# Four column groups for the weighted values, and layer norms worked out beside products, in an eight-stage kernel

## The chip, the cores and the metric

The kernel runs on one core of a Trainium2 chip. The metric is the device time of one launch in microseconds (us), median over runs. The core's engines are named as the profile names them: PE (TensorE; PEld is its loading of weights), DVE (VectorE), ACT (ScalarE), POOL (GpSimd) and SP, which issues the DMA transfers. Each engine works through its own list of instructions in order and waits only at semaphores.

## What is computed

The residual `x` holds 8 batches of 128 rows (tokens) of 512 columns. Four layers each add a gated attention and a gated feed-forward part, each over the layer norm of `x`:

```python
x = x + tanh(g_xattn[0]) * L0_xattn(layernorm(x), ctx, mask, ...)
x = x + tanh(g_ffn[0])   * L0_ffn(layernorm(x), w1, w2, w3)
x = x + tanh(g_xattn[1]) * L1_xattn(layernorm(x), ctx, ctx)
x = x + tanh(g_ffn[1])   * L1_ffn(layernorm(x), W_org, lora_down, lora_up, lora_keys, Wq)
x = x + tanh(g_xattn[2]) * L2_xattn(layernorm(x), ctx, Wq, Wk, Wv, Wo)
x = x + tanh(g_ffn[2])   * L2_ffn(layernorm(x), W_base, b_base, W_router, A, B)
# layer 3 in the same manner; the change does not touch it
```

The parts that the change touches, with their sizes:

- L0 attention (the "first attention"): 4 windows of 128 columns per batch, 8 heads of width 8; scores 128 x 128 per head and window, masked softmax, `o = attn @ v`, then gelu, an output projection 64 -> 128 and the mask.
- L0 feed-forward (the "first feed-forward stage"): `silu(h w1) * (h w2)`, then `@ w3`, hidden width 1376; only its end is touched.
- L1 feed-forward (the second): `h @ W_org` plus eight low-rank experts of rank 64; each batch's weights come from a softmax over the 8 expert keys for the mean row of that batch.
- L2 attention (the third): 16 query heads of width 96 over 4 key/value heads; keys and values from 128 context rows followed by the batch's own 128 rows ("latents").
- L2 feed-forward (the third): `h @ W_base + b_base` plus the two best of eight experts of rank 16.

## The kernel before

Eight stages run one after another, each a function; the change touches `l0_attention`, `l0_ffn`, `l1_ffn`, `l2_attention` and `l2_ffn`. Between stages all engines meet at a barrier and the semaphores are cleared. Most stages begin with `layernorm_all` (L129 to L214): it turns row statistics, which the stage before gathers behind each update of `x` (`row_stats`, L105), into means and variances of all eight batches (L135), takes the power -1/2 on POOL (L170), normalises on DVE, and, where the stage wants the rows transposed, has PE transpose each batch (L185, L194) and ACT copy it (L204). The order of work on each engine is written out by hand; `after(engine, semaphore, value)` is a wait.

**L0 attention.** A step works on batch b and prepares batch b + 1. PE projects queries and keys (`proj`, four tiles g), makes the scores twice: once with queries on the rows (`scores`, L411 and L416), from which DVE takes the maxima (L598), and once transposed (`scores_t`, L436 to L443), which ACT exponentiates (L527) into `pt`. The maxima are turned by PE (L423) and cast by DVE (L601), and that cast starts the next step's transposed scores. The weighted values are `pv` (L453): per head k and window n one product with a 128 x 128 weight tile, cut out of `vpad` so that head k's eight values and eight ones lie in the rows that belong to k; all heads add up in one bank, rows 0 to 63 numerators and 64 to 127 denominators. ACT copies the bank out (L542), and DVE takes reciprocals of 64 rows and multiplies (`second`, L571, L573), once per batch. `pt` has four slots, so later exponentials wait for `pv` of earlier heads. A last block takes gelu per batch, projects and updates `x`.

**L1 feed-forward.** Per pair of batches: POOL copies the transposed rows into `hs` (L1278), PE makes the low-rank "down" products per batch in 128 columns (L1290), the router's products (L1295, L1301), then the outputs (L1306 the base, L1309 the low-rank part) in 512 columns; DVE scales the low-rank values, updates `x` and gathers statistics.

**L2 attention.** A cycle of `step` handles the weighted values of batch b and the projections of b + 1. Weighted values (L1640): for each of four key/value heads r, four query heads g and two parts (context, latents), one product with the probabilities as 128 x 128 weights and 97 columns of values and ones; DVE takes four reciprocals and one product per r (L1815, L1817) into `o`, PE transposes `o` in twelve tiles (L1651), ACT copies them (L1737) to `o_t`, and the output products (L1661) follow. DVE also rounds the weights of the last stage here (`rounding`), beside everything else.

**L2 feed-forward.** Per batch four base products (L1957), one product of a row of ones with the bias (L1958), a transposition (L1960) and the expert product (L1962); POOL copies the rows (L1937) and, behind the last of these, scales weights of the next stage (L2065).

## Time and profile before

| | us |
|---|---|
| median of 3 runs | 1694.49 (1693.63 to 1696.26) |
| the profiled execution, its own time | 1687.38 |
| its span | 1685.6 |
| PE busy | 1444.7 |
| DVE busy | 1021.8 |
| ACT busy | 356.8 |
| POOL busy | 62.8 |

The span is what lies between the first and the last instruction. All starts below count from the span's start. A float32 product of PE stands as two instructions in the trace, so counts there are twice those of the code; their lengths are modelled and overlap, so a price is read from the start of one run of instructions to the start of the next. The stages lie at 24.1 to 233.4 (L0 attention, with its last block from 207.4), 247.8 to 616.2 (L0 feed-forward), 624.8 to 668.7 (L1 attention), 684.2 to 782.4 (L1 feed-forward), 796.5 to 1212.5 (L2 attention), 1229 to 1292.7 (L2 feed-forward), 1293.5 to 1543 and 1545 to 1682.5 (L3); the gaps are layer norms and barriers.

### The profile page before, as it was taken

Reading aid. Unit: us, or ns where it says so; the run is one execution under the profiler, and the core shown is the slowest. Engines: PE = TensorE matmul, PEld = TensorE weight load, DVE = VectorE, ACT = ScalarE, POOL = GpSimd, SP = SyncE. Lnnn points to the kernel's source line nnn. Section 1 sums busy time; section 2 is a strip of 40 time slices with the busy share of each in tenths; the row PEclk is TensorE's granted clock in tenths of the full one; section 3 lists DMA queues with packets and bytes.
Section 4 is the critical chain, followed back from the end, with each engine's and each line's share of the span. In section 5 each row is a group of like instructions: output and inputs, shape, how many; then the busy total and the mean of one; then the engine's idle time right before and its main releaser. Section 6 shows DMA issues by size and latency. Waiting matters only on the chain. (4 is left out here: it accounts for less than half of the span.)

```text
span 1685.6 us, 26597 instructions
## 1 busy us (share of the span) xinstructions
PE 1444.7 (86%) x8875; PEld 891.3 (53%) x8875; DVE 1021.8 (61%) x1652; ACT 356.8 (21%) x705; POOL 62.8 (4%) x100
## 2 busy tenths in 40 slices
PE   2989758999999966997999999999787789996575
PEld 1666623444444435665667777666443656652232
DVE  6577569778871137233566667666334256767886
ACT  1333321111113012101112121211111223332221
POOL 2000020000000000000000000000004000000000
PEclk9999858999999988898999999999698899998887
DMA  5000011011100037000000000000120000000000
GB/s 208 2 0 0 1 38 38 20 38 37 33 0 1 0 98 171 0 0 6 27 22 18 21 26 26 20 26 21 66 40 1 1 1 1 0 0 1 12 19 19
DMA packets 52311, 44.56 MB, mean 26 GB/s; under 512 B 38497, under 2 KB 38689, under 8 KB 51362
## 3 DMA queue, kind: packets, MB, share of 16 engines
q1 hardware_dynamic: 52258, 43.85, 8.8%
q8 instruction: 33, 0.54, 0.1%
q14 instruction: 20, 0.16, 0.0%
HBM read 41.74 MB, written 2.10 MB: 26 GB/s over the span
## 5 line engine op out<-in xcount | busy, mean ns | idle before, releaser
L932 DVE TENSOR_SCALAR f_side<-f_chunk 128x1536 f16<-128x1536 f32 x165 | 148.1, 955 | 46.1 <-PE f_sum L776 45.0
L776 PE MATMUL f_sum<-f_side,f_diag 128*128 128x512 f16 x495 | 122.2, 389 | 9.6 <-DVE f_side L932 8.1
L776 PEld LDWEIGHTS f_sum<-f_side,f_diag 128*128 128x128 f16 x495 | 47.9, 100 | 92.0 <-issue 45.0
L1573 PE MATMUL a_ps_b<-h_all,weights_a 128*128 (+1 forms) x768 | 92.1, 280 | 1.3 <-PEq L124 1.3
L1573 PEld LDWEIGHTS a_ps_b<-h_all,weights_a 128*128 128x128 f32 x768 | 89.1, 195 | 5.9 <-issue 5.9
L1661 PE MATMUL a_ps_y<-weights_a,a_o_t 128*128 128x512 f32 x192 | 89.3, 613 | 2.7 <-DVE a_v_ones L1793 2.0
L795 PE MATMUL f_gate<-h_all,f_w_t 128*128 128x512 f32 (+1 forms) x176 | 87.6, 598 | 0.0
L795 PE MATMUL f_up<-h_all,f_w_t 128*128 128x512 f32 (+1 forms) x176 | 79.6, 592 | 0.0
L847 PE MATMUL f_sum<-weights_a 128*128 128x512 f32 (+1 forms) x176 | 75.7, 592 | 0.0
L453 PE MATMUL a_o<-weights_a 128*128 128x128 f32 x512 | 70.1, 287 | 0.0
L453 PEld LDWEIGHTS a_o<-weights_a 128*128 128x128 f32 x512 | 62.7, 196 | 7.4 <-issue 3.5
L2237 PE MATMUL a_ps_a<-h_all,weights_a 128*128 (+1 forms) x512 | 64.1, 286 | 2.5 <-DVE a_sel L2482 2.5
L2237 PEld LDWEIGHTS a_ps_a<-h_all,weights_a 128*128 128x128 f32 x512 | 61.3, 200 | 9.2 <-issue 9.2
L2508 DVE TENSOR_REDUCE a_neg_max<-a_ps_a 128x8 f32<-128x1024 f32 x32 | 39.2, 1225 | 37.2 <-PE a_ps_a L2267 37.2
L1661 PEld LDWEIGHTS a_ps_y<-weights_a,a_o_t 128*128 128x128 f32 x192 | 35.6, 195 | 46.1 <-issue 45.9
L598 DVE TENSOR_REDUCE a_neg_max<-a_sa 128x8 f32<-128x1024 f32 x32 | 39.2, 1225 | 34.3 <-PE a_sa L416 34.0
L389 PE MATMUL a_proj<-h_all,a_wqk 128*128 (+1 forms) x64 | 36.6, 685 | 25.6 <-DVE a_neg_lo L564 24.1
L847 PEld LDWEIGHTS f_sum<-weights_a 128*128 128x128 f32 (+1 forms) x176 | 33.4, 190 | 42.2 <-issue 42.2
L1640 PE MATMUL a_ps_o<-a_v_ones,a_p_t_ctx 128*128 128x97 f32 x256 | 51.6, 285 | 4.0 <-DVE a_o L1817 3.2
L2416 ACT ACTIVATE a_p_t<-a_ps_st 128x512 f32<-128x512 f32 x64 | 34.8, 596 | 87.7 <-PE a_ps_st L2293 87.6
L170 POOL TENSOR_TENSOR ln_rstd<-ln_meanvar,ln_minus_half 128x8 f32<-128x8 f32 x7 | 11.6, 1652 | 1095.2 <-DVE ln_meanvar L137 1095.2
L795 PEld LDWEIGHTS f_up<-h_all,f_w_t 128*128 128x128 f32 (+1 forms) x176 | 32.8, 188 | 37.0 <-issue 35.6
(334 smaller groups left out, 2677.1 us busy)
## 6 DMA issues: line engine op xcount, KB each, us to landing
f_chunk<-in_l_w SPq DMA_DIRECT2D x30, 256.0 KB, 3.0
weights_a<-in_l_wgu SPq DMA_DIRECT2D x16, 232.0 KB
weights_a<-in_l_wq SPq DMA_DIRECT2D x48, 64.0 KB, 2.4
weights_a<-in_l_wo SPq DMA_DIRECT2D x1, 3072.0 KB, 11.6
weights_a<-in_l_wd SPq DMA_DIRECT2D x16, 192.0 KB, 3.1
x_res<-in_x SPq DMA_DIRECT2D x1, 2048.0 KB, 8.1
ctx_nat<-in_ctx SPq DMA_DIRECT2D x1, 2048.0 KB, 11.2
a_mask<-in_mask SPq DMA_DIRECT2D x1, 2048.0 KB, 15.7
```

What stands on the lines that cost most here:

```text
L389: nc.tensor.matmul(pproj[:, g % 2, :], wqk[:, g, :], h_n[:, bass.ds(b, 1), :].rearrange("p a n -> p (a n)"), start=True, stop=True).then_i ...
L453: mm = nc.tensor.matmul(po[:, c], vpad[:, s, n, k * P:(k + 1) * P], pt[:, k % 4, c], start=(k == 0 and n == 0), stop=(k == H0 - 1), skip_g ...
L598: nc.vector.tensor_reduce(to, psa[:, :, :].rearrange("p e (n j) -> p e n j", n=WN), AX.X, ALU.max, negate=True).then_inc(s_max, 1)
L776: mm = nc.tensor.matmul(psum[:, j, :], diag[:, k, :], side[:, k % RING, j * D:(j + 1) * D], start=(k == 0), stop=(k == LEVELS - 1), skip_g ...
L795: mm = nc.tensor.matmul((pg, pu)[w][0:r, g, :], wt[:, u, w, k, 0:r], h_t[:, k, g * D:(g + 1) * D], start=(k == 0), stop=(k == KT - 1), ski ...
L847: mm = nc.tensor.matmul(psum[:, i % 2, :], hid[0:r, t, i * P:(i + 1) * P], w3t[0:r, t, :], start=(t == 0), stop=(t == MT - 1))
L932: nc.vector.tensor_scalar(side[:, k % RING, :], wch[:, u, :], bounds[k], steps[k][0], ALU.is_le if k < ZERO else ALU.is_gt, ALU.mult).then ...
L1573: mm = nc.tensor.matmul(pb[:, u % 2, g * P:(g + 1) * P], wq_of(k, u, g), h_t[:, k, bass.ds(b * P, P)], start=(k == 0), stop=(k == KT - 1))
L1640: mm = nc.tensor.matmul(po[:, g * (HD2 + 1):(g + 1) * (HD2 + 1)], p, v[:, part, r, :], start=(part == 0), stop=(part == 1))
L1661: mm = nc.tensor.matmul(py[:, :], ot[:, t, :], wo[:, t, :], start=(t == 0), stop=(t == OT - 1))
L2237: mm = nc.tensor.matmul(pa[:, u // QG, (u % QG) * P:(u % QG + 1) * P], wq[:, k, u * P:(u + 1) * P], hb(b)(k), start=(k == 0), stop=(k == K ...
L2508: nc.vector.tensor_reduce(to, pa[:, :, :].rearrange("p e (i j) -> p e i j", i=QG), AX.X, ALU.max, negate=True).then_inc(s_max, 1)
```

## The change

It has five parts.

1. In L0 attention `pv` becomes `numerators` and `denominators`. Heads go in halves of four; head j of a half is a product with only 32 columns of weights and writes rows 32j to 32j + 31. Within these 32 rows two batches (s = 0, 1) and two halves have eight rows each, so the sums of two batches share one bank, and their denominators a second one, made on 512 columns with a small matrix of ones. DVE divides once per two batches, straight from the banks; the copy by ACT is gone. `pt` has eight slots, so exponentials wait for no weighted values. The order on PE and ACT is another (below); projections alternate between two banks; the values are added in two pieces, not four. The output weights come in 16 small transfers, the last block takes gelu per pair.
2. A class `NextNorm` gives the means, powers and normalised rows of the next stage's input batch by batch, behind each update. L0 feed-forward uses it for L1 attention, whose `layernorm_all` is gone; the loads for L1 feed-forward that stood there are issued in L0 feed-forward.
3. L1 feed-forward makes the down products on 512 columns for four batches at once, the router for all batches at once, reads the transposed rows where they are (no POOL copies), and ends with `NextNorm`, transposes and copies per batch, so that L2 attention's `layernorm_all` is gone.
4. L2 attention's weighted values become eight groups of four 32-column products on 512 columns (denominators, and three thirds u of the 96 values, each in two parts). They come out transposed, so the twelve transposes and three copies go; DVE takes one reciprocal of 128 x 512 and three products. The output weights are laid out for it by 16 transfers.
5. L2 feed-forward's bias product goes; DVE adds the gated bias, spread over 128 rows, to `x`.

```diff
 # l0_attention, PE
-                    def pv(b, s, k):
-                        if k == 0:
-                            after(pe, s_or, b + 1)
-                        after(pe, s_pt, b * 8 + (k + 1))
+                    def numerators(b, s, half, pair=None):
+                        if s == 0 and half == 0:
+                            after(pe, s_o, pair + 1)
+                        after(pe, s_pt, b * 8 + (4 * half + 4))
                         for n in range(WN):
                             c = slice(n * P, (n + 1) * P)
-                            mm = nc.tensor.matmul(po[:, c], vpad[:, s, n, k * P:(k + 1) * P], pt[:, k % 4, c],
-                                                  start=(k == 0 and n == 0), stop=(k == H0 - 1),
-                                                  skip_group_check=True)
+                            for j in range(4):
+                                k = 4 * half + j
+                                mm = nc.tensor.matmul(po[32 * j:32 * j + 32, c], v32[:, s, n, k, :], pt[:, k, c],
+                                                      start=(s == 0 and half == 0 and n == 0),
+                                                      stop=(s == 1 and half == 1), skip_group_check=True)
+                        mm.then_inc(s_pv, 1)
+
+                    def denominators(b, s, half):
+                        for j in range(4):
+                            mm = nc.tensor.matmul(pden[32 * j:32 * j + 32, :], ones32[:, s, half, :],
+                                                  pt[:, 4 * half + j, :], start=(s == 0 and half == 0),
+                                                  stop=(s == 1 and half == 1), skip_group_check=True)
                         mm.then_inc(s_pv, 1)
...
 # l0_attention, DVE
-                    def second(b):
-                        after(dve, s_or, b + 2)
-                        nc.vector.reciprocal(rec[:, :], oraw[64:128, :]).then_inc(s_rec, 1)
+                    def normalized(pair):
+                        after(dve, s_pv, pair * 8 + 8)
+                        nc.vector.reciprocal(rec[:, :], pden[:, :]).then_inc(s_rec, 1)
...
 # used by l0_ffn and l1_ffn behind each row_stats
+class NextNorm:
+    def meanvar(self, dve, b):
+        dve.wait_ge(self.chip.ln_sems["stats_ready"], self.base + b + 1)
+        nc.vector.bn_aggr(mv[:, b, :], self.chip.ln_stats[:, b, :]).then_inc(self.s_mv, 1)
+        dve.wait_ge(self.s_mv, 2 * b + 1)
+        nc.vector.tensor_scalar(mv[:, b, 1:2], mv[:, b, 1:2], EPS, None, ALU.add).then_inc(self.s_mv, 1)
+    def rstd(self, pool, b):
+        pool.wait_ge(self.s_mv, 2 * b + 2)
+        chip.nc.gpsimd.tensor_tensor(chip.ln_rstd[:, b:b + 1], chip.ln_mv[:, b, 1:2], chip.ln_mhalf[:, 0:1], ALU.pow)\
+            .then_inc(self.s_rstd, 1)
+    def normalized(self, dve, b, out):
+        dve.wait_ge(self.s_rstd, b + 1)
+        chip.nc.vector.tensor_scalar(out, chip.x[:, b, :], chip.ln_mv[:, b, 0:1], chip.ln_rstd[:, b:b + 1],
+                                     ALU.subtract, ALU.mult).then_inc(self.s_h, 1)
...
 # l1_ffn, PE
+                downs(0, (0, 1))
+                queries()
+                downs(0, (2,))
+                scores()
+                downs(0, (3,))
...
+                for b in range(NB):
+                    if b == HALF:
+                        downs(1, range(KT))
+                    outputs(b)
+                    if b:
+                        transposed(b - 1)
+                transposed(NB - 1)
...
 # l2_attention, PE
+                def weighted_values(b, first=False):
+                    after(pe, s_v, b * 2 + 2)
+                    after(pe, s_pt, b * 8 + 8)
                     if not first:
-                        after(pe, s_o, b * 4 + r)
-                    after(pe, s_pt, b * 8 + (5 + r))
-                    for g in range(G2):
-                        for part in range(2):
-                            p = pt1[:, r % 2, g * P:(g + 1) * P] if part else pt0[:, r, g * P:(g + 1) * P]
-                            mm = nc.tensor.matmul(po[:, g * (HD2 + 1):(g + 1) * (HD2 + 1)], p, v[:, part, r, :],
-                                                  start=(part == 0), stop=(part == 1))
-                    mm.then_inc(s_pv, 1)
+                        after(pe, s_rec, b)
+                    for out, of in [(po, lambda part, r: ones32[:, :])] + \
+                            [(pst[:, u, :], lambda part, r, u=u: v[:, part, r, 32 * u:32 * u + 32]) for u in range(U)]:
+                        for part, p in enumerate((pt0, pt1)):
+                            for r in range(KV2):
+                                mm = nc.tensor.matmul(out[row(r), :], of(part, r), p[:, r, :], start=(part == 0),
+                                                      stop=(part == 1), skip_group_check=True)
+                        mm.then_inc(s_pv, 1)
...
 # l2_ffn, PE and DVE
-                        nc.tensor.matmul(pout[:, u, :], ones[:, :], bias, start=False, stop=False)
...
+                        nc.vector.tensor_tensor(chip.x_at(b), chip.x_at(b), bias, ALU.add).then_inc(s_xb, 1)
```

On PE, in L0 attention's loop, this stands at the end of a step before; `a_sa` are scores, `a_o` the bank of weighted values, `a_mix` the bank in which the maxima are turned:

```order
L416 MATMUL a_sa<-a_qk 128x128 x8
L32 REGISTER_ALU
L453 MATMUL a_o<-weights_a 128x128 x8
L411 MATMUL a_sa<-a_mask_add,a_ones 128x512 x2
L416 MATMUL a_sa<-a_qk 128x128 x8
L32 REGISTER_ALU
L453 MATMUL a_o<-weights_a 128x128 x4
L411 MATMUL a_sa<-a_mask_add,a_ones 128x512 x2
L416 MATMUL a_sa<-a_qk 128x128 x8
L32 REGISTER_ALU
L453 MATMUL a_o<-weights_a 128x128 x4
L423 MATMUL a_mix<-ident,a_neg_max 128x128
```

and this in the same place of the changed kernel (`a_den` is the bank of denominators):

```order
L435 MATMUL a_mix<-a_wv,a_ctx_b 128x64 x4
L32 REGISTER_ALU
L496 MATMUL a_o<-weights_a 32x128 x16
L450 MATMUL a_sa<-a_mask_add,a_ones 128x512 x2
L455 MATMUL a_sa<-a_qk 128x128 x8
L503 MATMUL a_den<-weights_a,a_ones 32x512 x4
L32 REGISTER_ALU
L450 MATMUL a_sa<-a_mask_add,a_ones 128x512 x2
L455 MATMUL a_sa<-a_qk 128x128 x8
L32 REGISTER_ALU
L496 MATMUL a_o<-weights_a 32x128 x16
L450 MATMUL a_sa<-a_mask_add,a_ones 128x512 x2
```

All weighted values have moved behind the transposed scores, and a half's numerators or denominators stand between two rounds of scores; behind the last round of scores PE goes on, in the changed kernel, with the next batch's first projection and then the turning of the maxima.

On PE, in a cycle of L2 attention, before (`a_ps_o` the bank of weighted values, `a_p_t_ctx` and `a_p_t_lat` the probabilities of the two parts; the first two rows end the fourth of a cycle's blocks of weighted values, each of which has four such pairs; L1582 are keys, L1591 values, L1606 scores):

```order
L1640 MATMUL a_ps_o<-a_v_ones,a_p_t_ctx 128x97
L1640 MATMUL a_ps_o<-a_v_ones,a_p_t_lat 128x97
L1582 MATMUL a_ps_b<-ctx_tr,weights_a 128x128 x4
L1582 MATMUL a_ps_b<-h_all,weights_a 128x128 x4
L1582 MATMUL a_ps_b<-ctx_tr,weights_a 128x128 x4
L1582 MATMUL a_ps_b<-h_all,weights_a 128x128 x4
L1591 MATMUL a_ps_y<-weights_a,a_ctx_b 128x384 x4
L1651 MATMUL a_ps_b<-ident,a_o 128x128 x8
L1606 MATMUL a_ps_st<-a_k,a_q 128x256 x24
L1651 MATMUL a_ps_b<-ident,a_o 128x128 x4
```

and in the changed kernel, where the last two rows stand twice more behind these (L1662 is a tile of queries):

```order
L1662 MATMUL a_ps_b<-h_all,weights_a 128x128 x16
L1731 MATMUL a_ps_o<-a_p_t_ctx,a_ones 32x512 x4
L1731 MATMUL a_ps_o<-a_p_t_lat,a_ones 32x512 x4
L1731 MATMUL a_ps_st<-a_p_t_ctx,a_v 32x512 x4
L1731 MATMUL a_ps_st<-a_p_t_lat,a_v 32x512 x4
```

The four blocks that lay between queries and keys have become one block behind the first tile of queries, the two runs of transposes (L1651) are gone, and the numerators go into `a_ps_st`, the banks of the scores.

## Rows read from the trace of the kernel before

**Rows 1.** Busy time by stage: stretch, length, each engine's busy us, granted clock, DMA share, GB/s.

```profile
24.10:207.40 183.30, 157.81 (x1736) 117.14 (x1736) 117.11 (x160) 63.06 (x112) 0.00 (x0) 0.95 0.01 4
616.20:624.80 8.60, 0.00 (x0) 0.00 (x0) 5.17 (x18) 0.00 (x0) 1.72 (x2) 0.67 0.79 304
684.20:782.40 98.20, 94.70 (x464) 63.52 (x464) 29.77 (x72) 2.87 (x16) 4.22 (x7) 0.98 0.00 0
796.50:1212.50 416.00, 402.82 (x2920) 293.21 (x2920) 267.45 (x505) 79.28 (x152) 0.00 (x0) 0.96 0.07 22
1229.00:1292.70 63.70, 57.29 (x168) 27.45 (x168) 26.97 (x104) 4.27 (x16) 18.56 (x23) 0.96 0.04 6
```

**Rows 2.** Timeline, L0 attention: start, length, engine, line, operation, count, idle before and releaser.

```profile
41.89 0.29 DVE L601 CAST a_neg_max_t<-a_mix 128x128 bf16<-128x128 f32 x1 [0.63 <-PE a_mix L423]
98.62 2.05 PE L453 MATMUL a_o<-weights_a 128*128 128x128 f32 x16
101.37 1.23 DVE L598 TENSOR_REDUCE a_neg_max<-a_sa 128x8 f32<-128x1024 f32 x1 [1.30 <-PE a_sa L416]
103.51 1.22 DVE L598 TENSOR_REDUCE a_neg_max<-a_sa 128x8 f32<-128x1024 f32 x1 [0.91 <-PE a_sa L416]
187.27 0.29 DVE L601 CAST a_neg_max_t<-a_mix 128x128 bf16<-128x128 f32 x1 [0.48 <-PE a_mix L423]
188.52 1.08 ACT L527 ACTIVATE weights_a<-a_st 128x512 f32<-128x512 f32 x2 [1.04 <-PE a_st L443]
189.66 0.29 PE L436 MATMUL a_st<-a_qk 32*128 32x128 f16 x2 [1.18 <-ACT weights_a L527]
```

**Rows 3.** Timeline, L3 attention, the existing groups of four 32-column products.

```profile
1348.05 1.06 PE L2304 MATMUL a_ps_o<-a_p_t,a_v_pad 128*32 128x512 f32 x8
1348.50 0.13 PEld L2304 LDWEIGHTS a_ps_den<-a_p_t,a_ones 128*32 128x32 f32 x4 [0.30 <-issue]
1348.93 1.04 PE L2304 MATMUL a_ps_den<-a_p_t,a_ones 128*32 128x512 f32 x8
1349.90 0.23 PE L2267 MATMUL a_ps_a<-a_k_split,a_q_hi 32*128 32x128 f16 x2
```

**Rows 4.** Timeline, L1 feed-forward, PE: outputs of a batch.

```profile
702.61 3.60 PE L1306 MATMUL f_ps_out<-weights_b,f_h_b 128*128 128x512 f32 x8
706.04 3.60 PE L1309 MATMUL f_ps_out<-weights_b,f_hl 128*128 128x512 f32 x8
```

**Rows 5.** Timeline, L2 attention, PE: a cycle's block, its transposes, the last cycle.

```profile
936.99 0.36 PE L1640 MATMUL a_ps_o<-a_v_ones,a_p_t_ctx 128*128 128x97 f32 x2
938.75 0.41 PE L1573 MATMUL a_ps_b<-h_all,weights_a 128*128 x2
959.22 1.04 PE L1651 MATMUL a_ps_b<-ident,a_o 128*128 128x128 f32 x8
960.19 0.83 PE L1606 MATMUL a_ps_st<-a_k,a_q 32*128 32x256 bf16 x24
1177.95 0.43 PE L1640 MATMUL a_ps_o<-a_v_ones,a_p_t_ctx 128*128 128x97 f32 x2 [0.76 <-ACT a_p_t_lat L1732]
1198.08 1.19 PE L1661 MATMUL a_ps_y<-weights_a,a_o_t 128*128 128x512 f32 x1 [0.77 <-ACT a_o_t L1737]
```

**Rows 6.** Groups of instructions: line, engine, operation, tiles, count, busy us, mean ns, idle before.

```profile
L571 DVE RECIPROCAL a_rec<-a_o_raw 64x512 f32<-64x512 f32 x8 | 26.8, 3348 | 11.9 <-ACT a_o_raw L542 11.7
L2520 DVE RECIPROCAL a_rec<-a_ps_den 128x512 f32<-128x512 f32 x8 | 26.8, 3356 | 2.9 <-PE a_ps_den L2304 2.9
L2522 DVE TENSOR_TENSOR a_o_t<-a_ps_o,a_rec 128x512 f32<-128x512 f32 x8 | 5.5, 691 | 0.7
L1958 PE MATMUL f_ps_out<-f_bias,f_ones 1*128 1x512 f32 x16 | 9.0, 640 | 0.0
L2118 POOL TENSOR_TENSOR ln_rstd<-ln_meanvar,ln_minus_half 128x1 f32 x8 | 4.4, 544 | 229.8 <-DVE ln_meanvar L2112 229.8
```

**Rows 7.** Timeline, end of L2 feed-forward, POOL.

```profile
1276.74 14.46 POOL L2065 TENSOR_SCALAR weights_a<-f_raw_queries,weights_a 128x256 f32<-128x256 f32 x16
```

More of the change, by code:

```diff
@@ new lines, in step @@
+                        for m in range(H0 // 2):
+                            scores_t(b, s, m)
+                            if m < 3 and not last:
+                                proj(n, m + 1)
+                        if last:
+                            for half in range(2):
+                                numerators(b, s, half, pair)
+                                denominators(b, s, half)
+                            return
+                        v_proj(n)
+                        numerators(b, s, 0, pair)
@@ L1273, in _ @@
                 nc.gpsimd.memset(ones[:], 1.0).then_inc(s_c, 1)
[L1274 to L1278 removed]
+                for b in range(NB):
+                    norm.rstd(pool, b)
             @block.tensor
@@ L1364 @@
+                for part in range(2):
+                    for b in range(part * HALF, part * HALF + HALF):
+                        scaled(b)
+                    for b in range(part * HALF, part * HALF + HALF):
+                        updated(b)
 MXB = 32
```

596 lines of the change are left out of this document (295 added, 301 removed).

## The prediction

> **What bounds the kernel now.** I read the busy times by stage first [rows 1]. The reader is to see that TensorE (PE) is busy 402.8 of 416.0 us in the third attention, 94.7 of 98.2 in the second feed-forward stage and 57.3 of 63.7 in the third; that it does nothing in the 8.6 us between the first feed-forward stage and the second attention; and that in the first attention it is busy 157.8 of 183.3 with VectorE (DVE) at 117.1: there a chain of short waits between engines sets the pace. From 782.4 to 796.5, between the last two rows' stages, only a layer norm runs. So three things can pay: fewer PE issues where PE is full, shorter loops of waits in the first attention, and layer norms moved beside PE work. The change does all three. Then I read the timeline of one step of each stage [rows 2, 4, 5], and for the new form of product the one place where this trace already runs it [rows 3]. Last came the page's groups for prices [rows 6] and POOL's row at the end of the third feed-forward stage [rows 7].
>
> Every sum below is made in the profiled execution: 1687.4 us, 7.1 (0.4%) under the median of 1694.5; I add that back at the end.
>
> **First attention.** A step takes (187.27 - 41.89) / 7 = 20.77 us [rows 2]. A float32 product shows as two instructions, here called issues. Sixteen issues of the old weighted values, two heads, run from 98.62 in 2.0 us, so a batch's 8 heads x 4 windows, 64 issues, cost 8.0. The new form goes in groups of four 32-column products. A group on 512 columns issues in 0.88 (1348.05 to 1348.93) or 0.97 (1348.93 to 1349.90) [rows 3]; on 128 columns it is a quarter of it by columns, 0.22 to 0.30, an estimate. Per step that is 2 x 0.9 to 0.97 for denominators and 8 x 0.22 to 0.30 for numerators: 3.6 to 4.3 in place of 8.0. Not all of the 4 us comes back, since waits set the step. I walk the new step. First four rounds of transposed scores: from the end of the cast (187.56) exponentials start at 188.52, and the next round at 189.66, so a round is 2.1 and the last one 0.96: 7.3. The ACT copies go into the gaps behind each pair (a mean of 63.06 / 112 = 0.56 each [rows 1]) and would hide. Then the value projection, about 1.0 (estimate, from the 0.96 block). Then half 0's numerators, 1.0. Then four rounds of scores, each with a maximum: starts of maxima 101.37 and 103.51, so 2.14 each, 8.6. The other half's numerators and both denominators fit here in the 1.23 in which a maximum runs. About 0.9 more for turning the maxima and casting. Sum 18.8 for a plain step. On every second step DVE first does the joint reciprocal and product, 3.36 + 0.69 [rows 6], ahead of the casts of the projections; ACT's third biased copy waits for these, and exponentials queue behind it on ACT. That is 0.5 to 1.5 late, for three of seven steps. That the joint reciprocal on 128 rows costs no more than the old one on 64 (3356 against 3348 ns) makes it half as dear per batch. Mean step 19.2, gain 1.57 x 7 = 11. The last step, 187.3 to 207.4, becomes 7.3 + 1.3 (last exponentials) + about 4 (numerators, denominators) + 4.1 (reciprocal, product) = 16.7: gain 3. Together 14, between 4 (step at 20.2, last step unchanged) and 24 (17.9, last step 4).
>
> Loads of 32 columns: four show 0.13 us in all at 1348.50 [rows 3], so loads would not limit even a group of 0.22 to 0.30, eight loads at worst 0.26. The Trainium skill ("TensorE: Matmul & The Clock Gate", Part 3, Packing small matmuls) says that a weight load overlaps running products only when it is for another group of rows; groups of columns share their rows. By that rule short products wait for each load, which is the first rival below; the rows just named speak against it.
>
> **Layer norm ahead of the second attention.** The 8.6 us [rows 1] hold barrier, statistics, the power on POOL, and eight normalisations on DVE. New: batch by batch behind each update, hidden under the down products, save for the last: DVE's 5.17 over eight batches is 0.65, POOL's 128x1 power 0.54 [rows 6], handing over and barrier about 1.8 (estimate): 3.0. The loads of the next feed-forward stage, which SP issued in this gap (DMA share 0.79), go under the down products of the stage before. Gain 5.6, between 4.5 and 6.
>
> **Second feed-forward stage and the norm behind it.** Eight issues on 512 columns take 706.04 - 702.61 = 3.43 [rows 4], 0.43 each. New: 64 issues of down products 27.5, 128 of outputs 55.0, transposes 8 x 4 x 0.12 (eight take 0.97 at 959.22 to 960.19 [rows 5]) 3.9, router about 1: 87.4. From 684.2, with 2 for a slow start, PE ends at 773.6. Behind it come update, statistics, power 0.54, normalisation, four transposes and a copy, about 5, and barrier with three memsets 1.6: 780.2 instead of 796.5. Each batch's transposes are queued one output (6.9) behind it on PE, enough for the 3.4 of update, statistics and normalisation. Gain 16, between 12 (waits for the scaled low-rank values, which each output now shares) and 18.
>
> **Third attention.** Old per cycle: four blocks of 936.99 to 938.75 = 1.76, so 7.04, and twelve transposes 1.46 [rows 5]: 8.50. New: eight groups on 512 columns at 0.88 to 0.97: 7.04 to 7.76. So 0.74 to 1.46 per cycle; 1.1 x 7 = 7.7. DVE gets a 3.36 reciprocal and three products of 0.69, and loses smaller ones; at 267 of 416 us it has room, and the scores that reuse the numerators' banks stand behind the next batch's queries, values and keys on PE. The weighted values now wait for all exponentials of the batch, not a fourth of the last ones; one tile of queries (16 products of 128 columns, at the 1.76 / 8 = 0.22 of an old product 3.5 us) stands ahead as cover, and if it is short, PE loses the rest of one exponential, 0.6 at most, per cycle. In the last cycle, weighted values to output are 1177.95 to 1198.08, 20.1, because each block waits for DVE and the transposes and copies follow. New: 7.4 + the last product and hand-over 1 = 8.4; the reciprocal runs under the numerators. Gain 11.7 at most; if all of it ran half as fast, 16.8, it would be 3. The blocks with waits before are the nearer row to the first: I take 10.3. Together 18, between 0.74 x 7 + 3 = 8 and 1.46 x 7 + 11.7 = 22. The output weights now come in 16 transfers instead of one, long before their use: nothing.
>
> **Third feed-forward stage.** The bias products go: 16 issues with 9.0 us busy [rows 6], of which I take 8.4, since the end of one overlaps the next. DVE adds the bias instead, eight times about a product's 0.69, beside PE (27.0 busy of 63.7). POOL's last block (14.46 from 1276.74 [rows 7]) hangs on the same batches and moves along by seven eighths. 7.5, between 6 and 8.4.
>
> **Sum.** 14 + 5.6 + 16 + 18 + 7.5 = 61.1. Profiled 1626.3; as a median 1633.
>
> **Rivals.**
> 1. *Short products wait for their loads.* 32 issues of a half at 0.11 (a 512-column group's eight in 0.88 [rows 3]) are 3.5 instead of 1.0. One half stands on the path, the other overfills the maximum's gap: +4.5 a step, mean step 23.7, so 20 lost instead of 11 gained, and 2 more in the last: 1633 + 33 = 1666. For: no row has 32-column products on 128 columns. Against: 0.03 per load [rows 3]. Chance 0.11.
> 2. *Third attention's saving is hidden.* DVE's long reciprocal delays its queue (casts of queries, rounding), and the PE waits for these: cycles gain nothing and the last one 5: 1633 + 13 = 1646. Against: 267 of 416. Chance 0.08.
> 3. *Everything fits.* First attention's step at 17.9 (9 more), third attention with groups at 0.88 and its full last cycle (4 more): 1633 - 13 = 1620. Chance 0.06.
> 4. *Slower: the four products of a group run one after another.* In the third attention each group accumulates two parts into one bank, which rows 3 don't do. Eight issues at 0.43 are 3.4 instead of 0.92: 20 per cycle, 161 in eight; the time is about 1633 + 161 = 1794, more with the first attention. It decides from about 0.7 us excess on each of some 64 + 32 groups, a group of 1.6. Against: 0.88 in rows 3. Chance 0.03.
> 5. *It doesn't do what it says* (the chain of the norms isn't hidden, same time): 0.01.
>
> **How the numbers follow.** The forecast has 0.71. Its own range, with the terms' bounds partly cancelling, is 1618 to 1652; rivals 2 and 3 lie in it or at its edge, rival 1 mostly outside. For eight in ten I take 1616 to 1657. The runs shown differ by 0.15%, so 0.2% (3.4 us) is what can be told. Only rivals 4 and 5 are not faster: faster 0.96, same 0.01, slower 0.03.
>
> **What would show it.** In the profile after: start to start of the cast of maxima in the first attention 18.5 to 19.5 with longer and shorter steps alternating; numerators' 32 issues in about 1.0 us (3.5: rival 1); the second attention starting 3 us after the last down product's update; second feed-forward from 684 to 780; third attention's cycle 47.3 to 48.0 with groups at 0.9, its last weighted values to output 8 to 10; third feed-forward 7.5 shorter. The prediction is wrong if the granted clock falls inside the first attention's steps, or a new wait for DVE stands ahead of PE's scores in the third.

## The result, and the profile after

The changed kernel takes 1657.03 us (median of 3 runs, 1655.51 to 1657.41) against 1694.49 before: a ratio of 0.9775, 95% interval 0.9753 to 0.9797. In a second set of runs on another chip it is 0.9815 (0.979 to 0.9839). So it is faster by 2.3% in the first set and 1.9% in the second (by the intervals 2.0 to 2.5 and 1.6 to 2.1), at the very end of the predicted range and some 24 us short of the forecast.

Read by the last update of `x` of each stage, in the two profiled executions (1687.4 and 1657.0):

| stretch | before | after | difference | forecast |
|---|---|---|---|---|
| start of the span to the last update of L0 attention | 231.7 | 249.4 | +17.7 | -14 |
| layer norm ahead of L1 attention (last update to first DVE instruction of the stage) | 10.2 | 4.1 | -6.1 | -5.6 |
| L1 feed-forward, first product, to first product of L2 attention | 112.2 | 92.3 | -19.9 | -16 |
| L2 attention, first product to last update | 414.5 | 393.2 | -21.3 | -18 |
| L2 feed-forward, end to end | 80.1 | 72.8 | -7.3 | -7.5 |
| L3 attention (unchanged) | 250.2 | 256.5 | +6.3 | 0 |

Four parts gave 54.6 us where 47.1 were forecast. The first attention lost 17.7 where 14 were to be won. These 31.7 us are more than the whole shortfall of 30.7 in these two executions; the 7.5 that the other parts gave beyond the forecast and the 6.3 that L3 attention lost nearly cancel. First the stages after, in the columns of [rows 1] (stretch, length, busy us of PE, PEld, DVE, ACT and POOL, granted clock, DMA share, GB/s):

```profile
24.10:229.10 205.00, 175.67 (x1864) 95.16 (x1864) 100.86 (x136) 60.66 (x104) 0.00 (x0) 0.69 0.01 4
634.00:636.60 2.60, 0.00 (x0) 0.00 (x0) 0.90 (x4) 0.00 (x0) 0.70 (x2) 0.98 0.00 0
696.20:788.40 92.20, 87.44 (x234) 40.70 (x234) 29.52 (x57) 5.44 (x10) 4.80 (x11) 0.99 0.00 0
788.40:1182.40 394.00, 384.38 (x2824) 236.20 (x2824) 285.15 (x471) 63.83 (x128) 0.00 (x0) 0.99 0.08 23
```

The second row answers to the gap of 8.6 us, which is now 2.6; in the third and fourth PE is as full as before (87.4 of 92.2, 384.4 of 394.0), and they are shorter. In the first, the granted clock is 0.69; in the row of [rows 1] that answers to it it was 0.95. By step of the first attention, from one cast of the maxima to the next, in the changed kernel (four of the seven steps):

```profile
68.25:87.18 18.93, 15.41 (x233) 8.51 (x233) 10.58 (x16) 7.50 (x13) 0.00 (x0) 1.00 0.01 2
87.18:111.16 23.98, 21.59 (x233) 11.71 (x233) 14.58 (x19) 7.60 (x13) 0.00 (x0) 0.72 0.00 0
111.16:134.97 23.81, 21.43 (x233) 11.58 (x233) 10.67 (x16) 7.60 (x13) 0.00 (x0) 0.71 0.00 0
158.79:184.78 25.99, 25.11 (x233) 12.74 (x233) 10.67 (x17) 7.05 (x13) 0.00 (x0) 0.56 0.00 0
```

and a stretch of the kernel before, as long as one of its steps, in the same view:

```profile
83.40:104.20 20.80, 18.89 (x220) 14.21 (x219) 14.79 (x21) 7.80 (x14) 0.00 (x0) 1.00 0.00 0
```

The stretch before ran at clock 1.00, the upper level (2.4 GHz), as did six of the seven old steps. Of the seven new steps in this profile one ran there too, and it took 18.93 us: the walk in the prediction gave 18.8 for a plain step. The others took 23.8 to 26.0 us at 0.56 to 0.72. In a second profile of the same kernel (run 8 below) no step ran at 1.00; they took 23.0 to 25.2 us at 0.64 to 0.72. The first and the third of these rows hold the same instructions (233 on PE, none of them in a step with a joint reciprocal) and differ by 4.9 us and the clock alone. The second is a step with the reciprocal. In stretches of 2 us around the fall, with the same columns:

```profile
86.00:88.00 2.00, 0.95 (x16) 0.55 (x17) 1.41 (x3) 0.69 (x1) 0.00 (x0) 1.00 0.00 0
88.00:90.00 2.00, 1.70 (x21) 0.69 (x14) 2.00 (x1) 1.35 (x3) 0.00 (x0) 1.00 0.00 0
90.00:92.00 2.00, 2.00 (x25) 1.40 (x25) 1.76 (x3) 1.65 (x4) 0.00 (x0) 0.60 0.00 0
92.00:94.00 2.00, 2.00 (x20) 0.90 (x20) 1.71 (x4) 1.00 (x2) 0.00 (x0) 0.50 0.00 0
104.00:106.00 2.00, 1.92 (x46) 1.13 (x42) 1.00 (x2) 0.00 (x0) 0.00 (x0) 0.99 0.00 0
```

At 86 to 88 PE waits (0.95 busy of 2.00) for maxima, their turning and the cast; at 90 to 92 the clock is 0.60, and from 92 it is 0.50, the lower level (1.2 GHz). There PE is full (2.00 of 2.00), and at 104 the clock is back, to fall again in the next step (0.71 from 111 to 135). PE's waits from the start of the fast step to the fall, by what they wait for (us in total, times, longest):

```profile
PE a_sa L450 <- DVE a_neg_max L636: 1.6, 3, 0.5
PE a_st L475 <- ACT weights_a L567: 1.2, 4, 0.3
PE a_st L475 <- DVE a_neg_max_t L639: 1.2, 2, 0.6
PE a_mix L462 <- DVE a_neg_max L636: 0.5, 1, 0.5
```

None of these ten is longer than 0.6 us; together they are 4.5 of 23.75. In the kernel before, the step from 84.61 to 105.33 has four waits, 1.7 us in all. What the lower level costs shows in one run of numerators and the scores that follow it, at either level (start, length, engine, line, operation, count):

```profile
77.17 1.08 PE L496 MATMUL a_o<-weights_a 128*32 128x128 f32 x32
78.19 0.39 PE L450 MATMUL a_sa<-a_mask_add,a_ones 1*128 1x512 bf16 x2
...
99.79 1.94 PE L496 MATMUL a_o<-weights_a 128*32 128x128 f32 x32
101.66 0.61 PE L450 MATMUL a_sa<-a_mask_add,a_ones 1*128 1x512 bf16 x2
```

32 issues take 1.02 us at the upper level (77.17 to 78.19) and 1.87 at the lower. The same rows settle the first rival: at 1.02 the short products don't wait for their loads one after another; that would have been 3.5.

In the third attention, PE, a cycle's first two groups and the last cycle's first group and its output:

```profile
878.46 1.06 PE L1731 MATMUL a_ps_o<-a_p_t_ctx,a_ones 128*32 128x512 f32 x8
879.34 1.04 PE L1731 MATMUL a_ps_o<-a_p_t_lat,a_ones 128*32 128x512 f32 x8
...
1163.10 1.06 PE L1731 MATMUL a_ps_o<-a_p_t_ctx,a_ones 128*32 128x512 f32 x8 [2.18 <-issue]
1171.07 10.54 PE L1742 MATMUL a_ps_y<-weights_a,a_o_t 128*128 128x512 f32 x24 [0.90 <-DVE a_o_t L1879]
```

A group takes 0.88 and 0.86, so the fourth rival is gone; 1163.10 to 1171.07 is 8.0 us where [rows 5] had 20.1. The same two stretches in the columns of [rows 1], before and after:

```profile
1177.95:1198.08 20.13, 15.26 (x77) 13.79 (x77) 12.98 (x27) 3.31 (x6) 0.00 (x0) 0.61 0.00 1
1163.10:1171.07 7.97, 7.07 (x64) 2.38 (x65) 7.55 (x10) 0.00 (x0) 0.00 (x0) 1.00 0.01 2
```

So the old stretch was long not only for its waits and copies: its granted clock was 0.61, and the new one's is 1.00. The end of the second feed-forward stage:

```profile
782.59 0.75 DVE L1436 SCALAR_TENSOR_TENSOR x_res<-f_ps_out,tanh_g,x_res 128x512 f32<-128x512 f32 x1 [4.14 <-PE f_ps_out L1364]
785.81 0.66 PE L1379 MATMUL f_ps_norm<-ident,f_next_h 128*128 128x128 f32 x4 [2.82 <-DVE f_next_h L243]
788.45 1.83 PE L1662 MATMUL a_ps_b<-h_all,weights_a 128*128 128x128 f32 x7 [1.98 <-POOL a_ones L1618]
```

From the last update to the next stage's first product are 5.9 us, a layer norm, transposes and a barrier among them.

### The profile page after: what moved, and what is told of

Same layout as the page of the kernel before. It is cut to its first block and busy times, and to the rows that moved or that the text cites. A ratio compares the mean times of both kernels' runs of the same rounds, so it can differ in the third digit from the quotient of the medians.

```text
span 1655.2 us, 25190 instructions
## 1 busy us (share of the span) xinstructions
PE 1424.9 (86%) x8629; PEld 787.4 (48%) x8629; DVE 1020.9 (62%) x1580; ACT 330.4 (20%) x651; POOL 63.9 (4%) x108
## 5 line engine op out<-in xcount | busy, mean ns | idle before, releaser
L1662 PEld LDWEIGHTS a_ps_b<-h_all,weights_a 128*128 128x128 f32 x768 | 90.4, 196 | 14.4 <-issue 12.5
L1662 PE MATMUL a_ps_b<-h_all,weights_a 128*128 (+1 forms) x768 | 93.3, 281 | 2.0 <-POOL a_ones L1618 2.0
L817 PEld LDWEIGHTS f_sum<-f_side,f_diag 128*128 128x128 f16 x495 | 47.7, 99 | 91.3 <-issue 43.7
L836 PE MATMUL f_gate<-h_all,f_w_t 128*128 128x512 f32 (+1 forms) x176 | 87.4, 597 | 0.0
L1713 PE MATMUL a_ps_st<-a_q_t,a_k_t 32*128 32x512 f32 x384 | 48.7, 623 | 1.6 <-DVE a_neg_max_block L1866 0.8
L427 PE MATMUL a_proj<-h_all,a_wqk 128*128 (+1 forms) x32 | 27.1, 943 | 24.0 <-DVE a_neg_lo L601 24.0
L105 DVE BATCH_NORM_STATS2 ln_stats<-x_res 128x6 f32<-128x512 f32 (+1 forms) x56 | 38.2, 692 | 12.5 <-DMA gates<-in_g_ffn 7.2
L1860 DVE TENSOR_REDUCE a_neg_max<-a_ps_st 128x4 f32<-128x1024 f32 x32 | 37.7, 1219 | 12.0 <-PE a_ps_st L1695 12.0
L475 PE MATMUL a_st<-a_qk 32*128 32x128 f16 x256 | 34.0, 271 | 9.9 <-ACT weights_a L567 5.6
```

The source lines that it names most:

```text
L105: chip.nc.vector.bn_stats(chip.ln_stats[:, bass.ds(b, 1), :], chip.x_at(b)).then_inc(chip.ln_sems["stats_ready"], 1)
L817: mm = nc.tensor.matmul(psum[:, j, :], diag[:, k, :], side[:, k % RING, j * D:(j + 1) * D], start=(k == 0), stop=(k == LEVELS - 1), skip_g ...
L836: mm = nc.tensor.matmul((pg, pu)[w][0:r, g, :], wt[:, u, w, k, 0:r], h_t[:, k, g * D:(g + 1) * D], start=(k == 0), stop=(k == KT - 1), ski ...
L1662: mm = nc.tensor.matmul(pb[:, u % 2, g * P:(g + 1) * P], wq_of(k, u, g), h_t[:, k, bass.ds(b * P, P)], start=(k == 0), stop=(k == KT - 1))
L1713: nc.tensor.matmul(pst[:, r, :], kt[row(r), u, part * P:(part + 1) * P], qt[row(r), u, :], start=(u == 0), stop=False, skip_group_check=True)
L1860: nc.vector.tensor_reduce(to, pst[:, 2 * half:2 * half + 2, :] .rearrange("p r (e s) -> p r e s", e=2), AX.X, ALU.max, negate=True)\
```

## The experiments

**1. The old first attention put back into the changed kernel.** The function `l0_attention` is that of the kernel before; of its lines, those that set the order of products:

```diff
-                        numerators(b, s, 0, pair)
-                        scores(n, 1 - s, 0)
-                        denominators(b, s, 0)
-                        scores(n, 1 - s, 1)
...
+                        scores_t(b, s, 1)
+                        pv(b, s, 0)
+                        if not last:
+                            proj(n, 3)
+                        pv(b, s, 1)
+                        scores_t(b, s, 2)
```

> The changed kernel with the first attention of the kernel before put back; the other four parts stay. By the traces the new first attention lasts 17.7 us longer (steps +21.7, last block and ends -4), so both theories (clock, order) expect about 1639 us, 1634 to 1644. If the loss of some 5 us in the fourth attention, whose code is unchanged, comes from the first attention, it is 1634; if it comes from another part or from how the clock happens to stand there, 1639.

Measured: 1641.16 us, ratio to before 0.9714 (0.9667 to 0.9762). One of its steps:

```profile
84.94:105.83 20.89, 18.84 (x218) 14.16 (x218) 14.71 (x21) 7.87 (x14) 0.00 (x0) 1.00 0.00 1
```

Between the first step and the last, all take 20.6 to 20.9 at clock 1.00 again, and the last update is at 232.1. So without this part the change is better than with it: both theories expected that, and the sum of the other four is shown by itself.

**2. The new first attention alone, in the kernel before.** The reverse edit:

```diff
-                        pv(b, s, 0)
...
+                        numerators(b, s, 0, pair)
+                        scores(n, 1 - s, 0)
+                        denominators(b, s, 0)
...
```

> The kernel before with only the first attention of the changed kernel. If its loss is its own (clock theory), it loses 17 to 18 us against before whatever stands behind it: 1709 to 1713, ratio 1.009 to 1.011. If the low clock there needs something of the other parts (other loads, other order at the end), it is 1694 or below.

Measured: 1708.69 us, ratio 1.0125 (1.0094 to 1.0156): slower, by about as much as was expected of a loss of its own. Two of its steps:

```profile
113.51:137.33 23.82, 21.43 (x233) 11.48 (x233) 10.68 (x17) 7.60 (x13) 0.00 (x0) 0.71 0.00 0
137.33:161.24 23.91, 21.53 (x233) 11.56 (x233) 14.47 (x18) 7.60 (x13) 0.00 (x0) 0.71 0.00 0
```

23.8 and 23.9 us at 0.71, as in the changed kernel; the last update comes at 251.9. The loss is its own.

**3. Extra products in PE's waits.** They are made of constants and written to banks that are free at that time.

```diff
+                    def fill(bank, n):
+                        for e in range(n):
+                            nc.tensor.matmul(bank[:, e % 2, :], ones16[:, :],
+                                             sel8[:, 0:4, :].rearrange("p a n -> p (a n)"), start=True, stop=True,
+                                             skip_group_check=True)
...
                                 proj(n, m + 1)
+                                fill(psa, 2)
...
                         denominators(b, s, 0)
+                        after(pe, s_pt, b * 8 + 8)
+                        fill(pst, 2)
                         scores(n, 1 - s, 1)
                         numerators(b, s, 1)
+                        fill(pst, 2)
                         scores(n, 1 - s, 2)
                         denominators(b, s, 1)
+                        fill(pst, 2)
                         scores(n, 1 - s, 3)
                         if further:
                             proj(n + 1, 0)
+                        fill(pst, 2)
                         maxima_as_rows(n)
+                        fill(psa, 3)
```

> The changed kernel, with extra products of 512 bf16 columns in PE's waits of the first attention's steps: two behind each projection between rounds of transposed scores, two behind each score round, two and three around the turning of the maxima, into banks that are free there; their results are overwritten unread. Clock theory: the granted clock stays at the upper level in the steps, a step takes 18.9 to 19.6 instead of 23.9 us, the whole 1622 to 1630. Rival (the new order of products and waits is itself too long, the low clock beside the point): the extra products only add, step 24 to 26, the whole 1657 to 1670.

Measured: 1627.22 us, ratio 0.9618 (0.9572 to 0.9664). More work, and some 30 us less than the changed kernel (1.6 to 2.0% by the ratios). Two steps in a row, the first with the joint reciprocal:

```profile
88.87:108.47 19.60, 19.15 (x252) 9.76 (x251) 14.44 (x19) 7.33 (x13) 0.00 (x0) 1.00 0.00 0
108.47:127.58 19.11, 19.08 (x252) 9.73 (x251) 10.58 (x16) 7.55 (x13) 0.00 (x0) 1.00 0.00 0
```

Clock 1.00, 19.6 and 19.1 us. The kernel's own products stand in the same order as in the changed kernel, and none of their waits is gone; the wait for the last exponentials stands one round of scores earlier (the `after` in the diff), and in run 4, where it is back in its old place, steps of 19.1 occur too. The rival, that the order is itself too long, has fallen. The joint reciprocal costs 0.5 us a step at the upper clock. The first step, ahead of which nothing was added, still took 25.4 us at 0.72.

**4. Only those between rounds of transposed scores.** Against run 3:

```diff
                                 fill(psa, 2)
...
-                        after(pe, s_pt, b * 8 + 8)
-                        fill(pst, 2)
...
-                        fill(pst, 2)
+                        fill(pst, 0)
...
-                        fill(psa, 3)
+                        fill(psa, 0)
```

> As the run with all extra products, but only the two behind each of the three projections between rounds of transposed scores. Clock theory: it depends on whether that alone keeps the clock up: between 1622 and 1657, step 18.9 to 23.9, with the low stretches shorter than without. Rival (order): 1657 to 1662.

Measured: 1644.15 us, ratio 0.9729 (0.9681 to 0.9777).

```profile
86.41:111.69 25.28, 22.66 (x239) 11.72 (x239) 14.62 (x18) 7.60 (x13) 0.00 (x0) 0.73 0.00 0
111.69:130.81 19.12, 16.50 (x239) 9.01 (x239) 10.59 (x16) 7.55 (x13) 0.00 (x0) 1.00 0.00 0
```

Behind the first step (25.3 at 0.73), the three without the joint reciprocal stay up (19.1) and the three with it fall (24.5 to 25.3). Since the two kinds alternate, no run tells whether the reciprocal decides it or the step that went before; why the clock falls in the one and not in the other was not taken apart.

**5. Only those in the rounds of scores and at the turning of the maxima.** Against run 3:

```diff
                                 proj(n, m + 1)
-                                fill(psa, 2)
```

> As the run with all extra products, without the two behind each projection between rounds of transposed scores: they stand only in the rounds of scores and around the turning of the maxima. Clock theory: PE's waits there (0.5 us each at the upper clock) are as long as those between transposed scores; the clock stays up in most steps, at least in those without a joint reciprocal: 1628 to 1645. Rival (only the waits between transposed scores matter): as unedited, 1652 to 1659.

Measured: 1636.28 us, ratio 0.9688 (0.9662 to 0.9714). A step with the reciprocal and one without:

```profile
92.73:115.41 22.68, 20.58 (x244) 10.52 (x245) 14.53 (x19) 7.28 (x13) 0.00 (x0) 0.85 0.00 0
115.41:134.34 18.93, 17.67 (x244) 9.24 (x244) 10.57 (x17) 7.50 (x13) 0.00 (x0) 1.00 0.00 0
```

Again the steps without the reciprocal stay up (18.9; 19.6 at 0.97 the earliest), and those with it, 22.0 to 22.7 at 0.84 to 0.85, lie between run 4 and run 3. In the steps with the reciprocal both kinds of wait matter. The first step took 31.4 us at 0.50.

**6. One product at each place instead of two or three.** Against run 3:

```diff
-                                fill(psa, 2)
+                                fill(psa, 1)
...
-                        fill(pst, 2)
+                        fill(pst, 1)
...
-                        fill(psa, 3)
+                        fill(psa, 1)
```

> The changed kernel with the extra products at the same places as the run with all of them, but one at each place, 8 instead of 17 in a step. Clock theory: it lies between the unedited kernel (steps 23.9) and the run with all (19.1 and 19.6); if half is enough, steps 19 to 19.6 and the whole 1623 to 1630; if not, some steps fall low: 1632 to 1652. If the extra products worked by something else than keeping PE busy, the count would not matter.

Measured: 1630.74 us, ratio 0.9656 (0.9635 to 0.9677). The first step and two later ones:

```profile
42.49:73.51 31.02, 28.92 (x237) 15.07 (x241) 10.73 (x17) 8.15 (x14) 0.00 (x0) 0.50 0.01 1
92.44:112.05 19.61, 16.39 (x238) 9.21 (x241) 14.44 (x19) 7.28 (x13) 0.00 (x0) 1.00 0.00 0
112.05:130.98 18.93, 16.59 (x239) 9.21 (x241) 10.58 (x16) 7.49 (x13) 0.00 (x0) 1.00 0.00 0
```

One each is enough for the steps: with 8 products they are as long as with 17 (18.9 and 19.6 at 1.00). By the last sentence of the expectation this alone would also fit products that work by something else than keeping PE busy; run 7, in which PE has less to do and the clock falls, is what speaks against that. PE's waits in the second of these steps:

```profile
PE a_st L475 <- ACT weights_a L580: 1.3, 2, 1.0
PE a_sa L450 <- DVE a_neg_max L649: 1.2, 3, 0.5
PE a_st L475 <- DVE a_neg_max_t L652: 0.4, 1, 0.4
PE a_mix L462 <- DVE a_neg_max L649: 0.2, 1, 0.2
```

So the longest wait doesn't sort the steps: this one has seven waits, 3.1 us in all and one of 1.0, and stayed up, while the fast step of the changed kernel has eight, 3.6 in all and none over 0.6, and the clock fell behind it. The first step is at the lower level all through. It takes 31.0 us, as in run 5 and against 25.2 to 26.6 without extra products anywhere; that is not explained, and with it the whole lies between the two ranges expected.

**7. The kernel before with half of its weighted values left out.**

```diff
-                        for n in range(WN):
+                        for n in range(WN if k in (0, H0 - 1) else 2 if k in (3, 4) else 1):
                             c = slice(n * P, (n + 1) * P)
-                            mm = nc.tensor.matmul(po[:, c], vpad[:, s, n, k * P:(k + 1) * P], pt[:, k % 4, c],
+                            w = vpad[:, s, n, k * P:(k + 1) * P] if k else grp[:, :, :].rearrange("p q c -> p (q c)")
+                            mm = nc.tensor.matmul(po[:, c], w, pt[:, k % 4, c],
```

> The kernel before, with 16 of the 32 products of the weighted values of each batch of the first attention left out (and the first head's replaced by a product with a block matrix, so that every divisor is positive); its output is not the reference's. No column groups, order unchanged, 4.0 us less of PE work per step, as in the change. Clock theory: the work taken away is what kept the clock up; the clock falls within the steps as in the changed kernel and the time doesn't fall by the 2 to 4 us per step that the work would give, but stays about the same or rises: 1690 to 1725. Rival (the column groups, or the new order, bring the low clock or the longer step): clock at the upper level, step 17.5 to 20.5, the whole 1668 to 1692.

Measured: 1694.21 us, ratio 1.0015 (0.9994 to 1.0036): no difference. Two steps:

```profile
85.57:107.61 22.04, 20.12 (x186) 13.63 (x187) 14.62 (x21) 8.18 (x15) 0.00 (x0) 0.73 0.00 0
107.61:129.16 21.55, 19.54 (x186) 12.96 (x185) 14.53 (x21) 8.06 (x15) 0.00 (x0) 0.74 0.00 0
```

The clock, 1.00 before, is 0.73 and 0.74, the steps 22.0 and 21.6 instead of 20.8. There are no column groups and no new order here; 4 us of PE work less per step, as in the change, gain nothing, because the clock falls. The first head's products have other weights here, of the same size. This is the run that separates the causes most sharply.

**8. The changed kernel again**, without an edit, beside runs 2, 5 and 9.

> The changed kernel itself, unedited, to stand beside the others on one chip. Steps of the first attention 23.9 us with the granted clock between 0.5 and 0.75; the whole 1652 to 1659. The fourth attention, whose code the change leaves alone, took 256.6 us between the last updates of x in one profile and 252.8 to 252.9 in three kernels that differ from it only in the first attention: if that is chance of the clock, it is nearer 253 here; if the slow first attention causes it, 256 again.

Measured: 1657.28 us (ratio above), with no step of the first attention at 1.00. The fourth attention (L3) took 256.8. That spoke for the second reading, but run 6, whose steps are fast, has 256.4 there too, and run 4, half of whose steps are slow, 252.8. So neither reading holds: see the last section.

**9. More extra products, ahead of the first step and in the last.** Against run 3:

```diff
                             proj(b, g)
+                        fill(pst, 2)
                         v_proj(b)
+                        fill(pst, 1)
                         for m in range(H0 // 2):
                             scores(b, s, m)
+                            if m < 3:
+                                fill(pst, 3)
                         proj(b + 1, 0)
                         maxima_as_rows(b)
+                        fill(psa, 3)
...
+                            if m < 3 and last:
+                                fill(psa, 4)
```

> All extra products of before, and more of them ahead of the first step (three behind each round of scores there, three ahead of v_proj and scores) and four behind each round of transposed scores of the last step, which still began or went low. Clock theory: the first step falls from 25.4 to 19.5 to 22 us, the last loses 1 to 2: 1617 to 1625. Rival: the clock doesn't rise for it and the extra products only add at half speed: 1627 to 1633.

Measured: 1621.75 us, ratio 0.9592 (0.9568 to 0.9616). By the intervals the whole can't be told from run 3, which ran on another chip; the profiles tell more. The first step takes 22.3, and 22.1 and 19.2 in the next two runs with the same code there, against 25.2 to 31.4 in the seven profiles of the new first attention that have no extra products ahead of it. The last step, from its cast to its normalised values, here and in the changed kernel (the first row is of this run):

```profile
179.44:194.72 15.28, 10.34 (x190) 5.93 (x189) 4.33 (x3) 4.34 (x8) 0.00 (x0) 1.00 0.01 2
209.44:229.10 19.66, 11.57 (x176) 8.17 (x176) 4.33 (x3) 4.34 (x8) 0.00 (x0) 0.60 0.00 1
```

A second set of runs, without a further edit:

> The run with more extra products in the first attention, unedited, to stand beside the next one on the same chip: 1616 to 1624.

Measured: 1618.44 us, ratio 0.9591 (0.9569 to 0.9613).

**10. The same remedy at the start of the fourth attention,** whose code the change leaves alone: products of `ident16` with four copies of itself, two behind the keys, five behind each of three rounds of maxima ahead of the first step, four at their turning, and thirteen in the waits at the end of the first step. Against run 9:

```diff
+                    if not before:
+                        after(pe, s_ws, b * 4 + 4)
+                        fill(py, 3)
...
                 keys(0)
+                fill(pst, 2)
...
                     scores(0, 0, unit)
+                    fill(pst, 5)
                 maxima_as_rows(0)
+                fill(pst, 4)
```

> As the run beside it, with extra products of 512 bf16 columns also in the fourth attention: behind the rounds of maxima ahead of its first step and in the two waits at the end of the first step, where the granted clock is at 0.59 to 0.9 in these traces (in stretches of 10 us) and PE waits 1.3 us at a time. Clock theory: the stretches at half clock there get shorter, 253.5 us become 245 to 250, the whole 3 to 8 us less than the run beside it. Rival (the clock there is low because of what went before, the layer norm): no change, or 1 to 3 us more for the extra products.

Measured: 1612.77 us, ratio 0.9541 (0.9513 to 0.9568), beside 0.9591 for run 9 on the same chip. The fourth attention took 248.8 instead of 253.4 us, as expected. The first step of the first attention happened to stand at 1.00 in this profile (19.2 us, against 22.1 with the same code there), and the fourth attention lies anywhere from 250.2 to 256.8 in profiles without extra products there (last section). So the gain of the whole is shown, but how much of it belongs to the new products is not. This is the fastest version, 4.6% under the kernel before.

## Why the prediction was right and where it was wrong

The sign was right, the size not: 37.5 us of 61 by the medians, 30.4 by the profiled executions. That the time still lies at the end of the range is luck: the bounds of the first attention, a gain of 4 to 24, leave no room for a loss of 17.7, and the other parts made up 7.5 of it.

The step that failed is the term "First attention", 14 us, and within it not the walk but what it took for granted: "Mean step 19.2, gain 1.57 x 7 = 11" prices each round by rows of a step at the upper clock, with the work that kept it there taken out. At the upper clock the walk is right: 18.93 against 18.8, 19.1 to 19.6 with the extra products against 18.8 and 19.3 to 20.3. But six of the seven steps ran at 0.56 to 0.72, and the seven took 23.9 on average, (209.44 - 42.35) / 7, 3.1 more than the old ones. The forecast had named the case ("wrong if the granted clock falls inside the first attention's steps") without a price or a chance. It should have been a rival: by the prediction's own terms 4 of 8 us of products go and the waits stay, in a step that before had 18.9 us busy of 20.8. Runs 3 to 7 show that this is the cause: products that compute nothing bring the steps back to 19; products taken out of the old order, with no column groups and no new order, lower the clock there too.

The other terms, in the prediction's order. The last step was to win 3 and won 0.5 to its normalised values (20.1 to 19.6), at a granted clock of 0.60; in run 9 the clock is 1.00 there and the step takes 15.3, less than the forecast 16.7, so this part of the term failed by the clock too. The last block of the first attention won 4.1 more (26.0 to 21.9 us from its start to its last statistics), for which nothing was forecast. The traces show two differences there: with gelu per pair ACT loads its function table (ACT_TABLE_LOAD) once, not four times, at 1.28 us each, and the granted clock is 0.73 instead of 0.50; no run took them apart. The layer norm ahead of the second attention: 6.1 for 5.6. The second feed-forward stage: 19.9 for 16; PE ended at 782.4, 86.2 us behind its first product at 696.16 (forecast 89.4), and the next stage began 6.1 later (forecast 6.6). Third attention: cycles of 47.7 for 48.8, 1.1 each as forecast; the last cycle had 12.1 less from the weighted values to output where 10.3 were taken and 11.7 was the bound, and from the output's start to the last update it was 10.6 us for 12.9. Both are in part the clock's: the prediction put the old 20.1 down to waits, transposes and copies, but the granted clock was 0.61 there and 0.83 behind it, and 1.00 in both places of the changed kernel. No run tells how much. Against that, PE is idle for 2.2 us ahead of the last weighted values, 0.8 before. Third feed-forward stage: 7.3 for 7.5.

Of the rivals, the first, loads one after another, and the fourth, groups that run one product at a time, are refuted by the rows above (1.02 and 0.88). The first rival's mean step of 23.7 is nearly what was measured (23.9), but by another cause. The second didn't come about (21.3 gained), and in the third attention everything fitted, as in the third rival.

Two rules of the Trainium skill bear on this, both on the page "TensorE: Matmul & The Clock Gate". The one that the prediction weighed (Part 3, Packing small matmuls: loads overlap only for another group of rows) would have the short products wait for each load; the 1.02 us for 32 issues doesn't bear it out. The other (Part 1, A second HAM failure mode: psum-queue depth-cycling) tells of a kernel whose PE has short idle times between groups of products so often that its clock goes up and down between the two levels. The trace agrees: ten waits of at most 0.6 us, and the clock goes from 1.00 to 0.50 and back; but short waits alone don't sort the runs, since a step of run 6 with seven of them stayed up. By that rule the prediction would have had a rival on the slower side of its forecast.

## What to carry to other kernels

Work taken off PE is worth its time only if PE keeps its clock without it; in run 7, 4 us less a step gained nothing. Where a stage has many short waits and stands at the upper level, look at the granted clock and at PE's busy time there before counting any saving, and give the fall to the lower level a price of its own: here the same 32 issues took 1.87 us there and 1.02 above, and a step 23.8 instead of 18.9. A change made of several parts should be run part by part: here one of five was a loss of 1.25% that the other four hid.

## What the runs showed of the hardware

- Products that nothing reads made a kernel faster by 36 us (run 9 beside run 8): they stand in waits that were there anyway, and in the steps the granted clock is 1.00 instead of 0.7.
- The granted clock fell without any wait of PE over 0.6 us: in the step ahead of the fall PE was busy 15.41 of 18.93 us, in the stretch of the kernel before, which stayed up, 18.89 of 20.80. And it stayed up over a wait of 1.0 us in run 6, in a step of 19.61 us with 16.39 busy. Which property of PE's work decides is not shown.
- A reciprocal of 128 x 512 straight from a PSUM bank takes 3.36 us, in the changed first attention too, and one of 64 x 512 from SBUF 3.35 [rows 6].
- L3 attention, unchanged, took 256.4 to 256.8 us in four profiles (the changed kernel twice, run 2, run 6) and 252.8 to 253.5 in the seven profiles of other variants without extra products there; 250.2 in the kernel before. The clock in three stretches of it, in the changed kernel:

```profile
1314.00:1324.00 10.00, 6.58 (x57) 1.76 (x51) 4.37 (x4) 1.59 (x3) 0.00 (x0) 0.76 0.00 0
1324.00:1334.00 10.00, 10.00 (x68) 8.24 (x69) 4.05 (x2) 3.01 (x5) 0.00 (x0) 0.73 0.01 2
1364.00:1374.00 10.00, 8.84 (x71) 4.58 (x71) 3.70 (x6) 3.94 (x9) 0.00 (x0) 0.83 0.00 0
```

and in run 1, at the same distance from the stage's start within 0.3 us:

```profile
1297.00:1307.00 10.00, 6.58 (x61) 2.21 (x63) 4.87 (x6) 1.59 (x3) 0.00 (x0) 0.76 0.01 2
1307.00:1317.00 10.00, 10.00 (x84) 7.26 (x77) 4.05 (x2) 3.01 (x5) 0.00 (x0) 0.90 0.00 1
1347.00:1357.00 10.00, 8.84 (x79) 4.17 (x76) 4.54 (x6) 3.52 (x8) 0.00 (x0) 1.00 0.01 2
```

The second stretch is lower and the third falls once more. The instructions are the same, and neither the speed of the first attention nor the stage's start time sorts the profiles. What decides between these patterns is not known.
